# Perceiver block: context mixes in fours, and K's hi and lo parts made by DVE and POOL instead of ACT

## The reference

```python
Q = _proj(query, Wq, bq)           # query: layernorm(x), 256 x 512, 16 heads of 32
K = _proj(key, Wk, bk)             # key = value = ctx_1024, 25088 x 512
V = _proj(value, Wv, bv)
scores = jnp.einsum('bihd,bjhd->bijh', Q, K) * SCALE
attn = jax.nn.softmax(scores, axis=1)          # over the 256 queries, for each context row
x = jnp.einsum('bijh,bjhd->bihd', attn, V).reshape(B, S, D_MODEL)
return x @ Wo + bo
```

## Time and profile before

| | us |
|---|---|
| median of 3 runs (2762.91 to 2763.81) | 2763.53 |
| the profiled execution | 2764.92 |
| its span, first to last instruction | 2762.8 |
| of it, the loop over chunks: first scores 540.74, last mix near 2320 | 1779 |

### The profile page before, as it was taken

How to read it: one execution, slowest core, us unless ns; L and a number is a source line. 1 busy time by engine, 2 the same in 40 slices (tenths; PEclk the granted TensorE clock), 3 DMA queues, 4 the chain that set the end, 5 groups by cost and what they waited for, 6 DMA issues and landing times.

```text
span 2762.8 us, 58557 instructions
## 1 busy us (share of the span) xinstructions
PE 2683.4 (97%) x21096; PEld 2193.1 (79%) x21096; DVE 1962.2 (71%) x3791; ACT 2007.3 (73%) x7210; POOL 838.1 (30%) x1144
## 2 busy tenths in 40 slices
PE   7998999899999999999999999999999998999998
PEld 5776899777777777777777777777777775699997
DVE  6876866577777777777777777777777776655555
ACT  2112444299999999999999999999999996455553
POOL 4442111133333333333333333333333332222222
PEclk9999999999999999999999999999999999999999
DMA  8984454556665656666566656666656653445541
GB/s 330 381 332 170 171 196 172 145 139 157 157 161 152 158 150 154 162 159 151 146 165 161 153 151 158 152 161 153 159 151 151 165 138 127 155 179 192 185 183 69
DMA packets 132291, 473.26 MB, mean 171 GB/s; under 512 B 31128, under 2 KB 31256, under 8 KB 124832
## 3 DMA queue, kind: packets, MB, share of 16 engines
q1 hardware_dynamic: 131616, 468.47, 58.1%
q10 hardware_dynamic: 384, 1.05, 0.2%
HBM read 244.47 MB, written 17.30 MB: 95 GB/s over the span
## 4 chain that ended last, share of the span: by engine, by line
PE 84%; DVE 5%; POOL 5%; issue 2%; DMA 2%; ACT 1%; SPq 0%; POOLq 0%; DVEq 0%
PE PB L576 18%; PE PB L601 14%; PE PB L609 12%; PE PB L589 11%; PE PB L675 7%; PE PB L690 6%; PE PB L538 5%; PE PB L406 4%; POOL CTX L1440 3%; PE PB L551 2%; DVE small L1191 2%; DMA AR<-in_ctx 1%; POOL VS L1451 1%; DVE V L1187 1%; PE PB L434 1%
## 5 line engine op out<-in xcount | busy, mean ns | idle before, releaser
L817 ACT ACTIVATE EE<-PB,small 128x256 f32<-128x256 f32 x3136 | 1443.3, 482 | 132.2 <-DVE small L1191 117.6
L1191 DVE TENSOR_REDUCE small<-PB 128x2 f32<-128x512 f32 x1568 | 1062.7, 678 | 439.6 <-PE PB L601 439.0
L1451 POOL TENSOR_TENSOR VS<-V,small 128x128 f32<-128x128 f32 x784 | 346.9, 442 | 1207.9 <-DVE small L1197 1207.9
L817 ACT ACTIVATION_READ_ACCUMULATOR EE<-PB,small 128x1 f32 x3136 | 664.7, 213 | 0.0
L601 PEld LDWEIGHTS PB<-QS,STK 128*128 128x128 f32 x3136 | 480.3, 190 | 201.1 <-issue 162.2
L576 PE MATMUL PB<-CTX,WKV 128*128 128x256 f32 x4704 | 624.9, 282 | 2.9 <-POOL CTX L1440 2.9
L601 PE MATMUL PB<-QS,STK 128*128 128x256 f32 x3136 | 605.3, 295 | 4.9 <-ACT EE L817 3.2
L576 PEld LDWEIGHTS PB<-CTX,WKV 128*128 128x128 f32 x4704 | 588.8, 190 | 3.2 <-POOL CTX L1440 3.1
L589 PE MATMUL PB<-WKV,CTX 128*128 128x512 f32 x1584 | 433.7, 396 | 2.6 <-DVE V L1187 2.6
L609 PE MATMUL PB<-EE,VS 128*32 128x256 f32 x6272 | 426.7, 386 | 8.3 <-POOL VS L1451 8.3
L589 PEld LDWEIGHTS PB<-WKV,CTX 128*128 128x128 f32 x1584 | 274.0, 191 | 39.0 <-DVE V L1187 3.0
(11 more groups left out here) (198 smaller groups left out, 2485.4 us busy)
## 6 DMA issues: line engine op xcount, KB each, us to landing
STK<-KHL SPq DMA_DIRECT2D x1568, 128.0 KB, 2.9
RW<-in_l1f SPq DMA_DIRECT2D x32, 2048.0 KB, 8.1
AR<-in_ctx SPq DMA_DIRECT2D x49, 1024.0 KB, 8.7
RAW<-in_ctx SPq DMA_DIRECT2D x98, 512.0 KB, 4.2
WF<-in_l0f SPq DMA_DIRECT2D x17, 2304.0 KB, 8.8
v_scr<-RAW SPq DMA_DIRECT2D x64, 256.0 KB, 8.5
V<-v_scr SPq DMA_DIRECT2D x64, 256.0 KB, 2.9
WA<-in_l0a SPq DMA_DIRECT2D x1, 4096.0 KB, 12.5
```

Source lines behind the costliest of these rows:

```text
L817: m = e.activation(EE[:, b, s, :], bank(2 * (k % 2) + half, 256 * (s % 2), 256), ACT.Exp, bias=nm[:, b, s:s + 1], accum_out=su[:, b, s:s + 1])
L1191: e.tensor_reduce(nm[:, k % 4, 2 * half:2 * half + 2], bank(2 * (k % 2) + half).rearrange("p (s i) -> p s i", s=2), axis=AX.X, op=ALU.max, ...
L1451: e.tensor_tensor(VS[:, b, :].rearrange("p (s d) -> p s d", s=4), V[:, t % 4, 128 * c:128 * c + 128].rearrange("p (s d) -> p s d", s=4), r ...
```

## The change

- `mix` is called after every fourth chunk instead of every second: at k % 4 == 3 for the chunks k−5 to k−2 (`MIX = 4`). The buffers of exponentials, scaled V, maxima, sums and reciprocals grow from 4 to 6 (`RING = 6`).
- ACT no longer makes K's hi part in the loop. DVE copies K with its bias out of PSUM into a new tile `KR` of two buffers (`k_raw`), after the maxima and reciprocals of the same iteration. POOL casts it to hi one iteration later (`k_high`) and subtracts to lo another iteration later (`k_low`), both behind that iteration's `scale_v`. `project_k` waits for the copy instead of for `k_lo`, and `stack_k` for `k_low`.
- `split_hi` is done in two casts of 512 columns, at k % 8 == 4 and 5. `split_lo` is done in four subtracts of 256 columns: two at k % 8 == 5, one at 6, one at 7; `ctx_lo` rises with the last.
- `QHL` moves to share space with `WO`, which is loaded at chunk 40 instead of before the loop.

```diff
+MIX = 4
+RING = 6
...
+        def k_done(g, ch):
+            return ("k_lo", 4 * g + ch + 1) if g < 2 else ("kr_lo", 4 * (g - 2) + ch + 1)
...
             def stack_k(g):
-                w.wait_ge("k_lo", 4 * g + 4)
+                w.wait_ge(*k_done(g, 3))
...
                     g, ch = due_k(k)
-                    w.wait_ge("k_lo", 4 * g + ch)
+                    if k:
+                        w.wait_ge("kr_out", 4 * (g - 2) + ch)
                     project_k(g, ch)
...
-                if k % 2 and k >= 3:
-                    mix(k - 3)
-                    mix(k - 2)
+                if k % MIX == MIX - 1:
+                    for n in range(max(k - MIX - 1, 0), k - 1):
+                        mix(n)
...
             def exps(k, half):
-                b = k % 4
+                b = k % RING
                 w.wait_ge("s_max", 2 * k + half + 1)
-                if k >= 4:
-                    w.wait_ge("mix_mm", k - 3)
+                if k >= RING:
+                    w.wait_ge("mix_mm", k - RING + 1)
...
                 exps(k, 0)
-                if due_k(k):
-                    k_hi(*due_k(k))
                 exps(k, 1)
...
-            def split_hi(g):
+            def split_hi(g, parts=range(2)):
...
-                e.tensor_copy(CTX[:, g % 3, 0, :, :].rearrange("p c j -> p (c j)"), RAW[:, g % 3, :]).then_inc(S["ctx_hi"], 1)
+                for p in parts:
+                    e.tensor_copy(CTX[:, g % 3, 0, 2 * p:2 * p + 2, :].rearrange("p c j -> p (c j)"),
+                                  RAW[:, g % 3, 512 * p:512 * p + 512]).then_inc(S["ctx_hi"], 1)
...
+            def k_raw(g, ch):
+                n = 4 * (g - 2) + ch
+                w.wait_ge("kp_mm", 4 * g + ch + 1)
+                if n >= 2:
+                    w.wait_ge("kr_lo", n - 1)
+                e.tensor_scalar(KR[:, n % 2, :], bank(4, 0, GT), BC[:, C_L1XK + ch:C_L1XK + ch + 1], None,
+                                ALU.add).then_inc(S["kr_out"], 1)
...
             for k in range(NCH):
                 maxima(k, 0)
-                if k and due_k(k - 1):
-                    k_lo(*due_k(k - 1))
                 maxima(k, 1)
+                if k >= 1:
+                    reciprocals(k - 1)
+                if due_k(k):
+                    k_raw(*due_k(k))
                 if due_v(k) and due_v(k)[1] == 2:
                     v_out(due_v(k)[0])
-                if k >= 1:
-                    reciprocals(k - 1)
-                if k % 8 == 5 and k // 8 + 3 < NG:
-                    split_hi(k // 8 + 3)
+                if k % 8 in (4, 5) and k // 8 + 3 < NG:
+                    split_hi(k // 8 + 3, (k % 2,))
...
+            def split_lo(g, parts):
+                for c in parts:
+                    w.wait_ge("ctx_hi", 2 * g + c // 2 + 1)
+                    m = e.tensor_tensor(CTX[:, g % 3, 1, c, :], RAW[:, g % 3, GT * c:GT * c + GT],
+                                        CTX[:, g % 3, 0, c, :].bitcast(F32), ALU.subtract)
+                    if c == NC - 1:
+                        m.then_inc(S["ctx_lo"], 1)
...
+            def k_high(g, ch):
+                n = 4 * (g - 2) + ch
+                w.wait_ge("kr_out", n + 1)
+                if ch == 0:
+                    w.wait_ge(f"d_s{g % 2}", 256 * (g // 2))
+                e.tensor_copy(KHL[:, g % 2, 0, ch, :], KR[:, n % 2, :]).then_inc(S["kr_hi"], 1)
+
+            def k_low(g, ch):
+                n = 4 * (g - 2) + ch
+                w.wait_ge("kr_hi", n + 1)
+                e.tensor_tensor(KHL[:, g % 2, 1, ch, :], KR[:, n % 2, :], KHL[:, g % 2, 0, ch, :].bitcast(F32),
+                                ALU.subtract).then_inc(S["kr_lo"], 1)
+
+            split_lo(2, range(NC))
             for k in range(NCH):
                 if k >= 1:
                     scale_v(k - 1)
-                if k % 8 == 5 and k // 8 + 3 < NG:
-                    split_lo(k // 8 + 3)
+                if k >= 1 and due_k(k - 1):
+                    k_high(*due_k(k - 1))
+                if k >= 2 and due_k(k - 2):
+                    k_low(*due_k(k - 2))
+                if k % 8 >= 5 and k // 8 + 3 < NG:
+                    split_lo(k // 8 + 3, ((0, 1), (2,), (3,))[k % 8 - 5])
```

More of the change, by code:

```diff
@@ L43 @@
 f0_xs f0_xs_act f0_hi f0_lo f0_plo f0_up f0_silu f0_mul f0_hhi f0_hlo f0_dn f0_acc gate_mm gate_sig gate_comb
-ctx_hi ctx_lo kp_mm k_hi k_lo q_mm q_out q_split vp_mm v_out s_mm s_max s_exp s_rcp vs mix_mm ot_dve ot_act xo_mm x_xo x_xbias
+ctx_hi ctx_lo kp_mm k_hi k_lo kr_out kr_hi kr_lo q_mm q_out q_split vp_mm v_out s_mm s_max s_exp s_rcp vs mix_mm ot_dve ot_act xo_mm x_xo x_xbias
 f1_xs f1_xs_act f1_hi f1_lo f1_plo f1_up f1_gelu f1_hhi f1_hlo f1_dn f1_acc g1_mm g1_sub g1_exp g1_comb g1_turn g1_pt b2_mm b2_out f1_half x_lnb y_out
@@ L155, in build @@
         V = sb("V", [P, 4, D], over=life)
-        VS = sb("VS", [P, 4, P], over=life)
-        EE = sb("EE", [P, 4, 4, 256], over=life)
+        KR = sb("KR", [P, 2, GT], over=life)
+        VS = sb("VS", [P, RING, P], over=life)
+        EE = sb("EE", [P, RING, 4, 256], over=life)
         OT = sb("OT", [P, NC, 256], over=life)
+        q_life = ExitStack()
+        QHL = sb("QHL", [P, 2, NC, 256], F32R, q_life)
+        q_life.close()
         WO = sb("WO", [P, NC, D], over=life)
-        QHL = sb("QHL", [P, 2, NC, 256], F32R, life)
         life.close()
@@ L225, in build @@
         qf = EE[:, 3].rearrange("p c i -> p (c i)")
-        nm = small[:, 0:16].rearrange("p (b s) -> p b s", b=4)
-        su = small[:, 16:32].rearrange("p (b s) -> p b s", b=4)
-        rc = small[:, 32:48].rearrange("p (b s) -> p b s", b=4)
+        nm, su, rc = (small[:, o:o + 4 * RING].rearrange("p (b s) -> p b s", b=RING) for o in (0, 32, 64))
         KBANK = ((6, 2, 3, 7), (6, 2, 3, 4))
+        def k_done(g, ch):
+            return ("k_lo", 4 * g + ch + 1) if g < 2 else ("kr_lo", 4 * (g - 2) + ch + 1)
         WS1 = (WSA, WSB)
@@ L352, in sync_program @@
                     load_ctx(g + 6)
+                if k == 40:
+                    w.wait_ge("d_q", 256)
+                    e.dma_start(WO[:, :, :], a["l1x"][:, 2048:4096].rearrange("p (c n) -> p c n", c=NC)).then_inc(S["d_wo"], 16)
             def load_piece(n):
@@ L605, in mix @@
             def mix(k):
-                t, c, b = k // 4, k % 4, k % 4
+                t, c, b = k // 4, k % 4, k % RING
                 w.wait_ge("vs", k + 1)
@@ L805, in k_hi @@
                 w.wait_ge("kp_mm", 4 * g + ch + 1)
-                if g >= 2 and ch == 0:
-                    w.wait_ge(f"d_s{g % 2}", 256 * (g // 2))
                 e.activation(KHL[:, g % 2, 0, ch, :], bank(kb, 0, GT), ACT.Identity,
@@ L1167, in split_hi @@
                         w.wait_ge("vp_mm", v_count(2 * (g - 3) + 1))
[L1168 removed]
+                for p in parts:
+                    e.tensor_copy(CTX[:, g % 3, 0, 2 * p:2 * p + 2, :].rearrange("p c j -> p (c j)"),
+                                  RAW[:, g % 3, 512 * p:512 * p + 512]).then_inc(S["ctx_hi"], 1)
             def split_lo(g):
[L1171 removed]
+                w.wait_ge("ctx_hi", 2 * g + 2)
                 e.tensor_tensor(CTX[:, g % 3, 1, :, :].rearrange("p c j -> p (c j)"), RAW[:, g % 3, :],
@@ L1191, in maxima @@
                 e.tensor_reduce(
-                    nm[:, k % 4, 2 * half:2 * half + 2], bank(2 * (k % 2) + half).rearrange("p (s i) -> p s i", s=2),
+                    nm[:, k % RING, 2 * half:2 * half + 2], bank(2 * (k % 2) + half).rearrange("p (s i) -> p s i", s=2),
                     axis=AX.X, op=ALU.max, negate=True).then_inc(S["s_max"], 1)
@@ L1196, in reciprocals @@
                 w.wait_ge("s_exp", 2 * k + 2)
-                e.reciprocal(rc[:, k % 4, :], su[:, k % 4, :]).then_inc(S["s_rcp"], 1)
+                e.reciprocal(rc[:, k % RING, :], su[:, k % RING, :]).then_inc(S["s_rcp"], 1)
             split_hi(0)
@@ L1436, in gpsimd_program @@
                 rstd_of(3, i)
-            def split_lo(g):
-                w.wait_ge("ctx_hi", g + 1)
-                e.tensor_tensor(CTX[:, g % 3, 1, :, :].rearrange("p c j -> p (c j)"), RAW[:, g % 3, :],
-                                CTX[:, g % 3, 0, :, :].rearrange("p c j -> p (c j)").bitcast(F32),
-                                ALU.subtract).then_inc(S["ctx_lo"], 1)
+            def split_lo(g, parts):
[5 more added lines that the diff above has]
+                        m.then_inc(S["ctx_lo"], 1)
             def scale_v(k):
-                b, t, c = k % 4, k // 4, k % 4
+                b, t, c = k % RING, k // 4, k % 4
                 w.wait_ge("s_rcp", k + 1)
```

3 lines of the change are left out of this document (removed).

## The result

| us | before | after |
|---|---|---|
| median (lowest to highest) | 2763.67 (2762.91 to 2766.36) | 2849.49 (2847.14 to 2850.45) |
| ratio, 95% interval | | 1.031 (1.029 to 1.0325) |
| the profiled execution, its span | 2764.92, 2762.8 | 2850.01, 2848.3 |

What follows compares the result with a forecast made beforehand. The prediction took PE's stream in the 784-chunk loop as the bound: 2764.9 − 63 − 13 + 157 = 2846 us for the profiled execution, 2844.5 as median. Its range was 2776 to 2925.

Steps and rivals of the forecast that it cites:

- (1): PE's context mixes in blocks of four chunks: 191 blocks fewer at 0.33 us each, 63 us saved.
- Rival D: The 0.33 us belongs to each chunk's mixes, so fours save nothing: 2908 us, chance 0.03.
- (5): PE's K projection waits for POOL's last context lo part: 1.65 us at each of 95 boundaries, 157 us added.
- (2): POOL's context subtract in parts no longer delays scalings of V: 32 waits of 0.40 us, 13 us saved.
- (3): K leaves ACT, DVE copies it from PSUM; PE waits for that copy alone: taken as zero cost.
- (4): POOL's added work: K copy 0.40 us (0.31 to 0.74), subtract of 128x256 0.74 us, 0.70 in a row.
- T: Start of the first scores of a chunk whose number divides by 8; the prediction's times count from it.
- T': The prediction's time origin for stacks, counted from the delayed K projection; it put the last K subtract's end at T'+4.2.
- (6): Stacking DMAs on SP's queue start later, 0.4 us in hand on average; hidden by the stall, otherwise priced at 13 us.
- A: Rival: POOL meets its date for the last context part, so the change is faster: 2705 us, chance 0.13.
- B's floor: Rival: only DVE's chain sets the last context part's date, stall 0.95 us: 2778 us, chance 0.08.
- C: Rival: every second stall lowers PE's clock, 80 us on top: 2925 us, chance 0.14.

Runs made afterwards that it cites:

- The twos against the fours: The changed kernel with the context group's parts one iteration earlier, mixes in twos instead of fours: 2770.8 us against 2706.1 us.
- the fastest kernel: The changed kernel with K's lo part made right behind its hi part and the whole context split in iteration 3: 2683.9 us, ratio 0.971 to before.
- the first experiment: The changed kernel with the context group's hi and lo parts made one iteration earlier: 2706.1 us, ratio 0.980 to before.
- the best place of the split: Context split in iteration 3; there, K on ACT and DVE instead of DVE and POOL took 2739.3 us against 2683.9 us.
- the kernel without them: The changed kernel with parts one iteration earlier, plus K's lo subtract on POOL right behind its hi cast: 2706.3 us against 2706.1 us.
- the second 0.36 us copy: The changed kernel with two unused POOL copies instead of one ahead of each group's last K cast: 2980.1 us against 2889.0 us with one.

## Why the prediction was right

Against the profiled execution it said 2846; 2850 was measured. Its steps:

- **(1) Mixes in fours, −63.** The twos against the fours gave 64.6, or 0.34 us a block where 0.33 was read from rows 2 and 3. A period without a stall was to take 17.4 and takes 17.36 in the fastest kernel. Rival D is out. At the changed kernel's own places of the split a period without the stall takes 17.61, as the first experiment shows: the 0.25 us for exponentials at chunks 6 and 7 was put at nothing. It did not move the forecast, since the due time of (5) is an absolute one and swallows it.
- **(2) The subtract in parts, −13.** The 32 waits on a scaling are gone, as said. Of the two reasons given, fours alone do not do it (34 such waits stay with the whole subtract in iteration 5), and with twos a move of the subtract does not. With fours it goes by parts in iteration 5, and in iteration 3 also with a row of four subtracts (3.0 us).
- **(3) DVE copies K, zero.** No wait of K's projection on the copy is in the table, and the term stands. What it hides was not seen: with K left on ACT and DVE, fours take 55 us more at the best place of the split.
- **(4) POOL's durations.** The copy was taken at 0.40 and measured 0.397; the K subtract 0.78 on average (predicted 0.74) and the context subtract 0.75, with 0.70 from start to start in a row:

```profile
L1478 POOL CAST KHL<-KR 128x256 fp32r<-128x256 f32 x384 | 152.5, 397 | 0.0
...
L1483 POOL TENSOR_TENSOR KHL<-KR,KHL 128x256 fp32r<-128x256 f32 x384 | 300.6, 783 | 0.0
...
L1456 POOL TENSOR_TENSOR CTX<-RAW,CTX 128x256 fp32r<-128x256 f32 x384 | 283.0, 747 | 29.3 <-DVE CTX L1174 29.3
```

The estimate of 0.21 us plus a start for the copy, worked out from the rate that the Trainium skill gives one-input ops ("GPSIMD Engine Reference", section 4.1), is about half of the 0.397 measured; what it left open is the start, and that could be had from the rows. The subtract takes 0.742 us for 256 columns and 2.40 for 1024: 2.16 ns a column and 0.19 us that don't depend on the columns. By an estimate 0.21 + 0.19 is 0.40, as measured. With that start the trace agrees with the page, and the reason that the prediction gave for a sum 10 to 15 us smaller falls away. No run here has the copy in a second size, so its rate is not shown by itself.

- **(5) The due time, +157.** In the period shown T is 1248.10, which is 0.34 ahead of the delayed K projection at 1248.44, as the prediction counts T' (the scores themselves began at 1246.55). Chunk 4's reciprocal was to start at T+13.51 and starts at 1261.73, T+13.63; POOL's scaling at 13.76 and 13.87; its run of work was to take 5.44 and takes 1267.32 − 1261.97 = 5.35; the last part was to end at T+19.2 and ends at T+19.22. The stall, 1.65 us a period, is the difference of 19.03 (median) and 17.36 = 1.67; of it 1.43 lie at the K projection and 0.23 at the exponentials of chunks 6 and 7. The profile shows it as 1.2 to 1.4 us of waiting in 90 of the 95 periods. By the prediction's own dates the K projection would come 19.2 + 0.10 − 17.7 = 1.6 us late; its 1.65 counts from T+17.6. That 6 us too much was made up by the 0.14 behind the last part, where 0.10 was taken, and by the term left out.
  That term is `v_out`. In every third period DVE takes a V tile out of PSUM between the two half casts, and the second cast then falls beside POOL's first two subtracts, which take 1.61 us instead of 1.43:

```profile
1298.19 0.47 DVE L1174 CAST CTX<-RAW 128x512 fp32r<-128x512 f32 x1
...
1299.86 0.65 DVE L1202 TENSOR_TENSOR V<-PB,BI 128x512 f32<-128x512 f32 x1
1300.44 0.60 DVE L1174 CAST CTX<-RAW 128x512 fp32r<-128x512 f32 x1
1300.72 1.61 POOL L1456 TENSOR_TENSOR CTX<-RAW,CTX 128x256 fp32r<-128x256 f32 x2
...
1305.71 1.67 PE L584 MATMUL PB<-CTX,WKV 128*128 128x256 f32 x12 [1.39 <-POOL CTX L1456]
```

  Such periods take 19.2 instead of 19.0 us, 30 times, and make 6 of the 8 us by which the loop came out longer than 157 − 76 = 81.
- **(6) The stacks.** They start at T'+4.3 (predicted 4.2), take 12.6 us to the last landing (12.8), and land 0.8 us ahead of their use in the median (0.4 predicted on average); in 9 of 94 groups it is under 0.1, the scores having waited. The table shows 25 waits for them, 12 us. The price of 13 us without the stall was wrong: in the first experiment the same waits stand in the table, and the kernel without them is no faster (2706.3 against 2706.1).
- **The rivals.** A's time, 2705, is where the parts one iteration earlier led (2706.1): with the last part on time the change is faster, but in this kernel the condition was not met. That the two numbers agree is luck: A's sum has 13 + 5 = 18 us for late stacks and K's bank, neither of which any run shows, and in their place stand 0.25 × 95 = 24 us for exponentials. B's floor did not decide. C, the fall of the clock, did not happen in after (granted clock 1.00 in the loop, none of 95 waits followed by slow matmuls), but its place was found close by. One sign was off: PE's busy share in the loop was to fall to about 91% and is 279.8 of 300 us, 93%.

## What to carry to other kernels

Work that a transfer of buffers or a group boundary makes due belongs into the idle stretch of its engine, not behind the last thing that must be done in each step: reckon the due time of its last part by queue, op by op, and compare it with the time at which the consumer wants it. A gain in the bounding engine's stream (here 64 us by fewer changes of tile shape) brings all due times closer, so the slack of every side engine is to be worked out against the new, shorter period. And a stall that is a little too long has a second price when it lets the clock fall: here the second 0.36 us copy cost 91 us over 95 periods, 0.96 each.
